# Negated maxima as a DMA-joined row of stacks in two attention layers of a four-layer network on one Trainium2 core

## What is computed

```python
def _L2_attn_ref(x, w_qkv, w_out):            # 16 heads of 8, 256 tokens a sequence, causal
    q, k, v = jnp.split(jnp.einsum('bsi,oi->bso', x, w_qkv), 3, axis=-1)     # then to heads
    logits = jnp.einsum('bhsd,bhtd->bhst', q, k) * scale
    probs = jax.nn.softmax(jnp.where(mask, logits, neg_inf), axis=-1)
    ...
    return jnp.einsum('bsi,oi->bso', out, w_out)

def _L3_attn_ref(x, W_kv_down, W_k_up, W_v_up, W_q, W_q_rope, W_k_rope, W_o):
    ...                                       # 16 heads of 8 and a rotary part of 32 shared by all
    scores = jnp.einsum('bqhd,bkhd->bhqk', q, k)
    scores = scores + jnp.einsum('bqr,bkr->bqk', q_rope, k_rope)[:, None]
    w = jax.nn.softmax(jnp.where(causal[None, None], -jnp.inf, scores / scale), axis=-1)
    attn = jnp.einsum('bhqk,bkhd->bqhd', w, v).reshape(Bb, Tt, D_MODEL)
    return attn @ W_o

def _L3_ffn_ref(...):
    ...                                       # two of eight experts a token, and a shared part:
    shared = jax.nn.gelu(xf @ ws1 + bs1, approximate=False) @ ws2 + bs2
```

## Time and profile before

| | |
|---|---|
| median of three runs | 2612.24 us (2610.24 to 2615.01) |
| the profiled execution's own time | 2591.79 us |
| its span | 2590.0 us |
| mean granted TensorE clock | 0.879 of 2.4 GHz |
| busy share: PE, ACT, DVE, POOL | 78%, 61%, 61%, 44% |
| A2, first to last exponential of f32 | 1187.2 to 1599.5 us |
| A3, first to last exponential of f32 | 1832.9 to 2370.0 us |

### The profile page before, as it was taken

How to read it: one execution, slowest core, us unless ns; L and a number is a source line. 1 busy time by engine, 2 the same in 40 slices (tenths; PEclk the granted TensorE clock), 3 DMA queues, 4 the chain that set the end, 5 groups by cost and what they waited for, 6 DMA issues and landing times.

```text
span 2590.0 us, 66263 instructions
## 1 busy us (share of the span) xinstructions
PE 2029.6 (78%) x23246; PEld 1391.6 (54%) x23247; DVE 1579.7 (61%) x3648; ACT 1590.5 (61%) x3690; POOL 1141.4 (44%) x930
## 2 busy tenths in 40 slices
PE   1553899999999788437889886853899999997993
PEld 0223566666666566334555554633566666665662
DVE  2236788787887888764554454766444544443775
ACT  0231577676777455206988897530788888886552
POOL 0002577664555233314854554330466654333552
PEclk9785899999999899856787786985999999998997
DMA  8900000020000111200020000220000000000224
GB/s 224 170 0 0 12 17 17 18 77 3 2 2 2 41 46 47 82 24 14 22 67 2 2 2 6 53 62 8 11 17 18 16 12 2 2 2 10 64 62 124
DMA packets 109678, 88.19 MB, mean 34 GB/s; under 512 B 11240, under 2 KB 95816, under 8 KB 109424
## 3 DMA queue, kind: packets, MB, share of 16 engines
q1 hardware_dynamic: 97840, 60.82, 10.3%
q0 software_dynamic: 11584, 23.91, 2.7%
HBM read 45.26 MB, written 39.43 MB: 33 GB/s over the span
## 4 chain that ended last, share of the span: by engine, by line
PE 44%; DVE 21%; ACT 14%; issue 12%; POOL 6%; DMA 2%; DVEq 1%; SPq 1%; ACTq 0%; POOLq 0%
PE duo L1023 9%; PE mo L1023 9%; PE misc L1023 8%; PE ob L1023 6%; PE acc L1023 6%; PE pt L1023 4%; ACT qT L865 3%; POOL v L643 3%; ACT v L903 3%; ACT v L902 2%; DVE nmax L2084 2%; DVE v L1805 2%; DVE region L2087 1%; DVE nmax L1974 1%; ACT L902 1%
## 5 line engine op out<-in xcount | busy, mean ns | idle before, releaser
L643 POOL TENSOR_TENSOR v<-v 128x768 f16<-128x768 f32 x256 | 419.6, 1639 | 545.5 <-ACT v L903 544.4
L638 POOL TENSOR_TENSOR v<-v 128x512 f16<-128x512 f32 x256 | 290.3, 1152 | 259.2 <-DVE region L2087 259.0
L865 ACT ACTIVATE qT<-small_ident,nmax 128x128 f16<-128x128 f32 x1024 | 328.9, 404 | 58.7 <-DVE nmax L1974 57.5
L665 POOL DMA_INDIRECT results<-probT,dest_no x202 | 217.2, 1075 | 330.2 <-ACT probT L704 290.9
L1973 DVE TENSOR_REDUCE nmax<-duo 128x2 f32<-128x256 f32 x256 | 108.4, 423 | 391.5 <-PE duo L1023 391.1
L1023 PE MATMUL ob<-wm,v 128*128 128x9 f16 (+1 forms) x5856 | 255.8, 180 | 82.7 <-POOL v L643 62.9
L1023 PEld LDWEIGHTS ob<-wm,v 128*128 128x128 f16 x5856 | 222.7, 98 | 144.4 <-POOL v L643 84.3
L964 ACT ACTIVATE v<-mo 128x512 f32<-128x512 f32 x256 | 153.4, 599 | 159.3 <-PE mo L1023 159.3
L1023 PE MATMUL duo<-kT,wm 128*128 128x256 f16 x1212 | 173.3, 280 | 54.8 <-DVE kT L1793 28.8
L2084 DVE TENSOR_REDUCE nmax<-duo 128x2 f32<-128x512 f32 x256 | 164.8, 685 | 83.4 <-PE duo L1023 83.4
L1023 PE MATMUL mo<-qT,kT 64*128 64x256 f16 (+1 forms) x2240 | 200.6, 271 | 0.0
(11 more groups left out here) (279 smaller groups left out, 4726.6 us busy)
## 6 DMA issues: line engine op xcount, KB each, us to landing
prob<-slot_rows SPq DMA_DIRECT2D x101, 130.0 KB
qT<-results SPq DMA_DIRECT2D x40, 256.0 KB, 3.1
slot_rows<-prob SPq DMA_DIRECT2D x4, 1300.0 KB, 20.6
slot_rows<-prob SPq DMA_DIRECT2D x4, 1235.0 KB, 22.2
xd<-in_L_ffn_w_dram SPq DMA_DIRECT2D x2, 2048.0 KB, 12.1
results<-probT,dest_no POOLq DMA_INDIRECT x202
...
```

Source lines behind the costliest of these rows:

```text
L638: pool.tensor_tensor(p16[:, p % 2, h, 1, :], p32[:, h, :], p16[:, p % 2, h, 0, :], ALU.subtract)\
L643: pool.tensor_tensor(p16_2[:, p % 2, 1, :], p32_2[:, p % 2, :], p16_2[:, p % 2, 0, :], ALU.subtract)\
L665: pool.indirect_dma_start(out=results[layer], out_offset=bass.IndirectOffsetOnAxis(ap=dest_no[:, 2 * b + t:2 * b + t + 1], axis=0), in_=y_ ...
L865: ins = act.activation(diag2[:, p % 2, n // 2, n % 2, :], small_ident[:, :], ACT.Copy, scale=nmax4[:, p % 2, n:n + 1])
```

## The change

The diagonals, the selection products and the stack copies go. In their place:

- **Stacks by DMA.** SP's `feed_attention` fills each group's q and k stacks from `parts` by small DMAs from SBUF to SBUF (`refill`): 25 a group in layer 2 (24 of 8 rows and one of 4), 26 in layer 3 (24 of 8 rows and two of 104 rows by 4 heads). `parts` may be overwritten only when groups 2 and 3 have landed: `parts_free` on ACT and DVE, at step 3.
- **Maxima as a row.** The reductions write f16 (`nm16`). Every second step PE turns the maxima of two steps into 4 rows (`turn_maxima`, two products), DVE copies them to SBUF (`turn_rows`), and ACT issues a DMA of them into row 0 of each head's q stack (`send_rows`), where the k stack holds ones. So the product with the stack adds the maximum by itself.
- **Layer 3: one full product a head.** Each head gets a stack of 104 used rows of its own, rotary part, maximum and the head's rows together.
- **Order.** `maxima` runs 6 steps ahead in layer 2 and 4 in layer 3 (`LEAD`), and stands behind `average`. `prepare` moves to steps 3 to 8, the shared part to steps 9 to 13. The loads of layer 3's expert weights move into chunks 3 and 4 of A2.

```diff
-        SHARED_AT = {1: 0, 3: 1, 5: 2, 7: 3}
-        DOWN_AT = {4: 0, 5: 1, 7: 2, 8: 3}
-        PREPARE = range(9, 14)
+        SHARED_AT = {9: 0, 10: 1, 11: 2, 12: 3}
+        DOWN_AT = {10: 0, 11: 1, 12: 2, 13: 3}
+        PREPARE = range(2, 10)
+        LEAD = {2: 6, 3: 4}
+        REFILL = {2: 25, 3: 26}
+        REFILL_AT = {2: {6: (0,), 8: (1,), 12: (2,)}, 3: {8: (0, 1), 12: (2,)}}
+        HEAD0 = 96
+
...
+        def rows_ahead(layer, p, more):
+
+            e = (p + LEAD[layer] - 2) // 2
+            if p % 2 or e < 0:
+                return None
+            return (0, e) if e < 8 else (1, e - 8) if more else None
...
+            def feed_attention(layer):
+
+                stage = f"A{layer}"
+                stage_closed(sp, f"T{layer}")
+                sp.wait_ge(stack_set, layer - 1)
+
+                def refill(i, g):
+
+                    if i:
+                        s_full.wait(sp, stage, i - 1, 8 * g + 7)
+
+                    def put(dst, src):
+                        sp.dma_start(dst, src).then_inc(stack_in[g], 16)
+
+                    if layer == 2:
+                        put(q_stack[0:P:GROUP, g, :], k_stack[1:5, 0, :])
+                        for j in range(4):
+                            own = parts[GROUP * g + 8 * j:GROUP * g + 8 * j + 8, :, :]
+                            for stack, rows in ((k_stack, (2, 2, 3)), (q_stack, (0, 1, 0))):
+                                for r, n in enumerate(rows):
+                                    at = GROUP * j + 8 * r + 8
+                                    put(stack[at:at + 8, g, :], own[:, n, :])
+                    else:
+                        for stack, rope, rows in ((head_k[g], after["k"][0], (2, 2, 3)), (head_q[g], after["q"][0], (0, 1, 0))):
+                            put(stack[0:HEAD0 + 8, :, :],
+                                rope[0:HEAD0 + 8, :].rearrange("p (o c) -> p o c", o=1).broadcast_to([HEAD0 + 8, 4, CHUNK]))
+                            for j in range(4):
+                                own = parts[GROUP * g + 8 * j:GROUP * g + 8 * j + 8, :, :]
+                                for r, n in enumerate(rows):
+                                    at = HEAD0 + 8 + 8 * r
+                                    put(stack[at:at + 8, j, :], own[:, n, :])
+
+                after = kept[layer]
+                prepared = 1 if layer == 2 else 11
+                proj_read_v.wait(sp, stage, 0, prepared)
+                for g in range(4):
+                    refill(0, g)
+                for i in range(NCH):
+                    if i:
+                        refill(i, 3)
+                    if layer == 2 and i == 3:
+                        sp.wait_ge(rows_sent[2], 16 * ALL * TOP[2])
+                        load_up(xd_flat, A["L3_ffn_w1"], exp_in[3])
+                    if layer == 2 and i == 4:
+                        load_down(load2[:, :], A["L3_ffn_w2"], exp_in[3])
+                    if i < NCH - 1:
+                        proj_read_v.wait(sp, stage, i + 1, prepared)
+                        for p in sorted(REFILL_AT[layer]):
+                            for g in REFILL_AT[layer][p]:
+                                refill(i + 1, g)
+
             def feed_experts(layer):
...
-            sp.wait_ge(rows_sent[2], 16 * ALL * TOP[2])
-            stage_closed(sp, "T2")
-            load_up(xd_flat, A["L3_ffn_w1"], exp_in[3])
-            load_down(load2[:, :], A["L3_ffn_w2"], exp_in[3])
+            feed_attention(2)
             feed_experts(2)
             feed_combine(2)
+            feed_attention(3)
             feed_experts(3)
...
+                def send_rows(i, e):
+
+                    g, b = e // 2, e % 2
+                    nm_turned.wait(act, stage, i, e)
+                    own = slice(SEQ * b, SEQ * (b + 1))
+                    if layer == 2:
+                        act.dma_start(q_stack[0:P:GROUP, g, own], nm_rows[:, b, :]).then_inc(nm_in[b], 16)
+                    else:
+                        act.dma_start(head_q[g][HEAD0:HEAD0 + 1, :, own], nm_rows[:, b, :]).then_inc(nm_in[b], 16)
+
...
                         .then_inc(v_high.sem, 1)
 
                 def prepare(i, parity, p):
 
                     if layer == 2:
-                        if p == 11:
+                        if p == 3:
+                            parts_free(i)
                             high(i, 0, 0, acc, SCALE2)
-                            high(i, 2, 1, misc, 1.0)
...
-                        elif more:
-                            diagonals(i + 1, p + 2 - STEPS)
+                        exps(i, p, 0)
+                        at = rows_ahead(layer, p, more)
+                        if at:
+                            send_rows(i + at[0], at[1])
+                        exps(i, p, 1)
...
+
+                nm_bank = [misc[0:4, 0:P], misc[0:4, P:SEQ]] if layer == 2 else                     [duo[0:4, 0, LINE:CHUNK], duo[0:4, 1, LINE:CHUNK]]
+
+                def turn_maxima(i, e):
+
+                    nmax_made.wait(pe, stage, i, 2 * e + 1)
+                    if layer == 2:
+                        at_step(nm_turned, pe, stage, i, e - 1)
+                    for qt in range(2):
+                        ins = mm(nm_bank[qt], nm16[:, e % 2, 4 * qt:4 * qt + 4], ident_h[:, :], True, True)
+                    ins.then_inc(nm_full.sem, 1)
+
+                def maxima(i, p):
 
                     g, b, jj = pair2(p)
                     if p % 4 == 0:
-                        stacked.wait(pe, stage, i, 2 * g + 1)
+                        pe.wait_ge(stack_in[g], stack_count(layer, i + 1))
                     at_step(nmax_made, pe, stage, i, p - 1)
+                    if layer == 3 and p % 2 == 0:
+                        at_step(nm_turned, pe, stage, i, p // 2 - 1)
...
-                            r = head(g, jj, h)
-                            mm(duo[:, h, P * qt:P + SEQ * qt], q_stack[r, g, q0 + P * qt:q0 + P * qt + P],
-                               k_stack[r, g, k0:k0 + P + P * qt], layer == 2 and qt == 0, False)
+                            q, k = rows_of(g, jj, h)
+                            mm(duo[:, h, P * qt:P + SEQ * qt], q[:, q0 + P * qt:q0 + P * qt + P], k[:, k0:k0 + P + P * qt],
+                               qt == 0, False)
                     for h in range(2):
-                        mm(own_tiles(duo[:, h, 0:LINE]), ident16[:, :], twice(mask16[:, :]), False, True)                            .then_inc(max_full.sem, 1)
-
...
-                        if layer == 3:
-                            q, k = after["q"][parity], after["k"][parity]
-                            mm(dst[:, 0:SEQ], k[:, k0:k0 + P], q[:, q0:q0 + SEQ], False, False)
-                            mm(dst[:, SEQ:LINE], k[:, k0 + P:k0 + SEQ], q[:, q0 + P:q0 + SEQ], False, False)
                     for kt in range(2):
                         for h in range(2):
-                            r = head(g, jj, h)
-                            ins = mm(trio[(2 * p + h) % 3][:, SEQ * kt:SEQ + P * kt],
-                                     k_stack[r, g, k0 + P * kt:k0 + P * kt + P], q_stack[r, g, q0 + P * kt:q0 + SEQ],
-                                     False, kt == 1)
-                            if kt:
-                                ins.then_inc(s_full.sem, 1)
+                            u = 2 * p + h
+                            if kt == 0:
+                                at_step(p_high, pe, stage, i, u - 3 if u >= 3 else u - 2)
+                            q, k = rows_of(g, jj, h)
+                            mm(trio[u % 3][:, SEQ * kt:SEQ + P * kt], k[:, k0 + P * kt:k0 + P * kt + P],
+                               q[:, q0 + P * kt:q0 + SEQ], kt == 0, False)
...
+                        scores(i, p)
+                        at = rows_ahead(layer, p, more)
+                        if at:
+                            turn_maxima(i + at[0], at[1])
                         if p >= 1:
                             average(i, parity, p - 1)
                         elif begun:
                             average(i - 1, 1 - parity, STEPS - 1)
+                        at = ahead(layer, p, more)
+                        if at:
+                            maxima(i + at[0], at[1])
                         if begun and p == 1:
                             turn_o(i - 1)
...
+                blank_rows = (k_stack[:, :, :], q_stack[:, :, :]) if layer == 2 else \
+                    (after["k"][0][HEAD0:P, :], after["q"][0][HEAD0:P, :])
+                for a in blank_rows:
+                    dve.memset(a, 0.0).then_inc(stack_zero, 1)
+                dve.wait_ge(stack_zero, 2 * (layer - 1))
+                if layer == 2:
+                    for j in range(4):
+                        ins = dve.memset(k_stack[GROUP * j:GROUP * j + 1, :, :], 1.0)
+                else:
+                    ins = dve.memset(after["k"][0][HEAD0:HEAD0 + 1, :], 1.0)
...
 
                     if layer == 2:
-                        if p == 11:
```

(19 more changed lines are left out.)

276 lines of the change are left out of this document (134 added, 142 removed).

## The result

The changed kernel takes **3096.76 us** (median of four runs, 3090.13 to 3100.32), the kernel before on the same chip 2611.46: a ratio of **1.185** (1.183 to 1.188). The forecast was 2704, range 2590 to 2780. The sign was right, the size was not: +485 us in place of +92.

A forecast was written before the change was run, and what follows sets the result against it. It took ACT to bound A2's undisturbed steps, and a loop of two steps to bound the changed kernel; 14 + 18 + 16 + 24 + 20 = +92 us on the median of 2612.2 gave 2704 us, range 2590 to 2780.

The forecast's parts named there:

- What bounds the kernel: Before the change: ACT sets an undisturbed step of A2, 2.65 us of exponentials and diagonals without a gap.
- the loop of two steps: Plain steps of A2 and A3: waiting for the row of maxima makes a pair take 6.20 us and 6.16 us.
- ACT's issue: ACT's DMA of the maxima between the two heads' exponentials: 0.36 us, bounds 0.2 and 0.63.
- What stands on top: Work per chunk beyond the loop: 4.1 us in layer 2; 21.6 in layer 3, 10.6 in its last chunk.
- The Gelu part: Layer 3, steps 9 to 12: ACT is the limit, five steps go from 15.4 to 24.2 us, +8.8 a chunk.
- The granted clock: PE's clock: A2 at 1.2 GHz for 40% of the time, +16 us; A3 kept at 1.00.
- a rival came true: A3 loses its clock, 40% of the time at 1.2 GHz: 2751 us, chance 0.18.
- SP's DMAs in the steady state I cost at nothing: Stack refills in A2 and A3: SP's issues, 36 and 39 us a chunk, stay hidden behind the slow loop.
- the text's own ring: SP's issuing, landing and the projections it waits for: closes in 43 of some 55 us in A2, 56 of 71 in A3.
- SP is the limit: Rival: at 0.63 us an issue the ring takes 70 us in A2, 82 in A3; 2911 us, chance 0.06.
- Starts: First exponentials of A2 and A3 delayed by memsets, issues and maxima: +24 us and +20 us.
- Moved rotations: Layer 3, step 7: DVE's 2.5 us of work delays the row copy, +2.1 us a chunk.

The follow-up runs named there:

- rows32: The changed kernel with stacks refilled by fewer DMAs of more rows, 7 a group in layer 2 and 8 in layer 3; 2649.9 us, ratio 1.025.
- late_rot: rows32_send_late with DVE's rotations in layer 3 a step or two later and four one-row memsets made one; 2542.8 us, ratio 0.984.
- late_rot_fill: late_rot with three unread PE products of 256 columns added to each step of layer 2; 2546.2 us, ratio 0.984.
- rows32_send_late: rows32 with ACT's DMA of the rows issued behind the second head's exponentials; 2582.9 us, ratio 0.998.

## Why the prediction was wrong

**What bounds the kernel, and the loop of two steps: right.** In rows32, where SP is free, the pair of plain steps in A2 takes 6.86 us at 1.2 GHz against the 6.20 + 0.6 forecast. Its parts: the turn 0.37 (0.37), the copy 0.41, with the signal 0.47 (0.47), ACT's issue 0.52 (0.36). Taking the DMA out of the way gave 1.04 back. That kernel is 64 us slower than before, where the sum said 92; that the two are near is in part luck, for the terms below miss in both directions.

**What stands on top: somewhat too much in both layers.** In rows32 an inner chunk of A2 takes 57.8 us, and eight pairs of 6.86 are 54.9: 2.9 on top, 4.1 in the forecast. The stage is 41 us longer than before, against +14 and +16, because the low clock lasts nearly all of it. An inner chunk of A3 takes 67.2; eight of the forecast's pairs of 6.16 would leave 17.9 of it for what the forecast put at 21.6, but no plain pair of A3 was timed. A3 is 11 us shorter than before where +18 stood. The Gelu part measured 21.3 us for five steps (4 x 4.95 and 1.50), 24.2 in the forecast.

**The granted clock: the term was too small, and a rival came true.** A2 was put at 40% of the time at 1.2 GHz; it ran at 0.52 in the changed kernel, nearly all of it, though PE was 68% busy there (390 of 570 us). A3, kept at 1.00, fell to 0.74, and in late_rot it is 0.91. The rival asked 47 us for that. In rows32, at 0.86, A3 is shorter than before all the same; its condition came, and its price can't be read, for no run has A3 with the clock kept. The Trainium skill (TensorE: Matmul & The Clock Gate, Part 1) has a less busy PE put back to 1.2 GHz; A3's fall from 1.00 agrees, and so does late_rot_fill, where added products brought A2 from 0.58 to 0.71.

**"SP's DMAs in the steady state I cost at nothing": the step that failed.** It rested on the price of one issue, 0.36 us, from two DMAs of 8 rows, nearest in shape, with 0.63 as the upper bound from the row below. The changed kernel's DMA of 8 rows takes 0.625 us and 0.04 to the next. The number of rows was not the likeness that counts: 32 rows take 0.594 here, no more than 8. The two in the earlier trace rows load from DRAM, where these go from SBUF to SBUF; that this makes the difference is likely, but no run tests it. With 0.667, the text's own ring comes out as it was measured in A2: 66.7 of issuing and some 7 for projections and landing, 73.4 us a chunk. The text even named the point: "it decides from 0.47 an issue", and 0.47 lay well within its bounds of 0.36 and 0.63. A chance of 0.06 for a price whose bounds lie on both sides of the deciding point was too low, and the range should have reached 2911.

**The rival "SP is the limit" had the mechanism and was 186 us short.** A2: 3.4 us a chunk from 0.63 to 0.667. A3: it put the ring at 82, measured are 103.5. Two terms were short. The second DMA behind each broadcast of 104 x 4 rows takes 1.6 to 1.8 in place of 0.625, so that a stack is 10.05 us and not 13 x 0.63 = 8.2, 15 us a chunk. And the part that SP waits for is 21.6 us, not 15 and 2, because it runs through steps 4 to 8 of the loop.

**Starts: right in kind, short by the same price.** A2 began 50 us later, where +24 stood. 10.7 of them come from ahead of the stage, where no instruction was changed (in rows32 the same place comes 3.6 us earlier than in the kernel before, so this is spread between executions). The four one-row memsets cost what was said (1.76 each, 8.9 with gaps); the two groups of 25 issues that the first scores need take 33 us, where the forecast's price gives 18.

**Moved rotations.** The forecast charged step 7 with 2.1 us for DVE's 2.5 us of work. It cost more than twice that, in step 8 (8 to 9 us in rows32_send_late, 4.0 in late_rot), because the forecast took DVE's prices from the earlier trace rows, at the stage's start, where GpSimd's subtraction doesn't run: one operation of 0.70 there took 2.59 beside it.
